# Layer 1's experts in two 64-column halves with 68 streamed columns, issued two experts ahead

## The reference, cut to what matters

```python
E = 32; K = 2; CF = 1.2; D = 128; F = 512
C = int(math.ceil(T * K / E * CF))                  # 68 slots for each expert
xe = jnp.zeros((E, C, D), x.dtype).at[flat_e, pos_d].add(x_rep, mode='drop')
he = jax.nn.gelu(jnp.einsum('ecd,edf->ecf', xe, w1) + b1[:, None, :], approximate=False)
ye = jnp.einsum('ecf,efd->ecd', he, w2) + b2[:, None, :]
y_flat = ye[flat_e, jnp.minimum(pos, C - 1)] * valid[:, None].astype(x.dtype)
y = (y_flat.reshape(T, K, D) * w[..., None]).sum(axis=1)
```

## Time and profile before

| | us |
|---|---|
| median of 3 runs | 669.22 |
| lowest, highest | 668.12, 670.95 |
| span of the profiled execution, first to last instruction | 666.6 |
| median less that span | 2.6 |
| PE busy | 527.9 (79%) |
| DVE busy | 386.9 (58%) |
| ACT busy | 328.5 (49%) |
| POOL busy | 219.3 (33%) |
| first L1667 matmul starts | 571.98 |
| last L1677 matmul ends | 639.36 |

### The profile page before, as it was taken

The page is one execution under the profiler, slowest core; times in us unless marked ns, Lnnn a source line. Parts: engine busy times, 40 slices in busy tenths (PEclk is TensorE's granted clock), DMA queues, the critical chain, the costliest instruction groups (busy, mean ns, idle before and its releaser), DMA issues.

```text
span 666.6 us, 15622 instructions
## 1 busy us (share of the span) xinstructions
PE 527.9 (79%) x5272; PEld 403.1 (60%) x5272; DVE 386.9 (58%) x1148; ACT 328.5 (49%) x953; POOL 219.3 (33%) x409
## 2 busy tenths in 40 slices
PE   2968878876879996999999998999997720799930
PEld 1623245544744535788888887888886420799930
DVE  1699845557365543777877877787786350122212
ACT  2646734344121223887787877778785210222210
POOL 8384722124100000534344443444433016000025
PEclk9798977899868997999999999999999575699985
DMA  9985543333199925000004999000001971200012
GB/s 275 232 236 144 156 155 110 98 113 92 33 233 225 207 72 224 2 2 3 1 0 107 228 230 179 2 2 1 0 0 32 425 304 51 68 17 17 17 36 67
DMA packets 46839, 73.32 MB, mean 110 GB/s; under 512 B 4613, under 2 KB 40374, under 8 KB 45638
## 3 DMA queue, kind: packets, MB, share of 16 engines
q1 hardware_dynamic: 42588, 59.93, 35.9%
q0 software_dynamic: 1472, 8.72, 3.6%
q10 hardware_dynamic: 2730, 4.03, 2.0%
HBM read 69.06 MB, written 3.60 MB: 109 GB/s over the span
## 4 chain that ended last, share of the span: by engine, by line
PE 49%; DVE 20%; ACT 11%; DMA 6%; issue 6%; POOL 6%; POOLq 1%; ACTq 0%; SPq 0%; DVEq 0%
PE ps L1541 9%; ACT work L833 6%; PE ps L1555 5%; PE ps L1677 4%; PE ps L1478 4%; PE ps L1667 4%; DMA work<-in_kv_blk 3%; PE ps L1512 2%; PE ps L1586 2%; POOL xe_scratch L720 2%; DVE ps L1164 2%; DVE sumsq L958 2%; POOL early_w L725 2%; PE ps L1415 2%; PE ps L1358 2%
## 5 line engine op out<-in xcount | busy, mean ns | idle before, releaser
L833 ACT ACTIVATE work<-ps,nb,rkey 125x56 f32<-125x56 f32 x576 | 176.3, 403 | 52.1 <-DVE nb L1167 44.9
L1541 PE MATMUL ps<-work,region 128*64 128x96 f32 (+1 forms) x2304 | 116.7, 252 | 7.0 <-DVE work L1227 4.8
L1541 PEld LDWEIGHTS ps<-work,region 128*64 128x64 f32 (+1 forms) x2304 | 99.5, 137 | 18.7 <-issue 5.2
L1555 PE MATMUL ps<-region,work 125*64 125x129 f32 x1152 | 72.5, 273 | 4.6 <-POOL work L686 3.1
L686 POOL TENSOR_TENSOR work<-work,rs 125x336 f32<-125x336 f32 x96 | 71.9, 749 | 7.5
L1555 PEld LDWEIGHTS ps<-region,work 125*64 125x64 f32 x1152 | 64.1, 136 | 5.4 <-POOL work L686 3.6
L684 POOL TENSOR_TENSOR rs<-rs,rkey 125x6 f32<-125x6 f32 x96 | 19.2, 201 | 123.8 <-DVE rs L1179 123.8
L1164 DVE TENSOR_REDUCE ps<-ps 125x6 f32<-125x336 f32 x96 | 48.9, 510 | 17.9 <-PE ps L1541 17.4
L1175 DVE TENSOR_REDUCE sm<-work 125x6 f32<-125x336 f32 x96 | 47.4, 494 | 1.2 <-ACT work L833 0.6
L725 POOL DMA_INDIRECT early_w<-ys_scratch,gidx x14 | 13.4, 958 | 83.3 <-DMA ys_scratch<-folded 79.4
L1386 PE MATMUL ps<-xln,folded 128*128 128x448 f32 x64 | 29.9, 592 | 9.5 <-ACT region L760 9.5
(11 more groups left out here) (296 smaller groups left out, 1037.9 us busy)
## 6 DMA issues: line engine op xcount, KB each, us to landing
region<-in_w SPq DMA_DIRECT2D x6, 2048.0 KB, 19.5
region<-in_ctxT SPq DMA_DIRECT2D x16, 750.0 KB
early_w<-in_ctx SPq DMA_DIRECT2D x16, 672.0 KB
region<-in_ctx SPq DMA_DIRECT2D x16, 672.0 KB
work<-in_ctxT_blk SPq DMA_DIRECT2D x22, 187.5 KB
early_w<-in_w POOLq DMA_DIRECT2D x1, 4096.0 KB, 12.4
region<-in_ctx_blk ACTq DMA_DIRECT2D x11, 187.5 KB
early_w<-in_ctx_blk ACTq DMA_DIRECT2D x10, 187.5 KB
```

The lines of the kernel that those rows point to most:

```text
L833: i = act.activation(shares_of(a, h)[:, c, :], ps[:CP, 2 + 2 * a + h, c * S:(c + 1) * S], ACT.Exp, bias=nb[:, a, q:q + 1], scale=rkey[:, b ...
L1541: mm = pe.matmul(ps[r0:r1, 2 + 2 * a + h, c * S:c * S + WIDE], keysT[:, s, c0 + r0:c0 + r1], qT[:, p, a * S:a * S + WIDE], start=True, sto ...
L1555: mm = pe.matmul(ps[i * COL:(i + 1) * COL, bank, 0:KW], A[:CP, i, h, c * S:c * S + COL], keys[:, 2 * p + i, h * CH + c, :], start=(h == 0 ...
```

## The change

The weights of both products are split in two column halves: each matmul becomes two of 64 weight columns, the first writing PSUM partitions 0 to 63 and the second 64 to 127. Each streams the expert's own 68 columns, so the zeroed pads and POOL's three memsets and the wait for them (`wide_ok`) go. `hidden` runs two experts ahead in three banks (0, 1, 4), and the order is the same for all experts. The transposed token chunks use banks 5 and 7. DVE's sum of a group is taken out two experts later, and `slot_rows` and its copy stand two experts later as well. DVE's and ACT's instructions keep their shapes.

```diff
+HBANK = (0, 1, 4)
+XBANK = (5, 7, 5, 5, 5)
@@ POOL
-            gp.wait_ge(ln_out, 8)
-            gp.memset(xeT[:, SLOTS:], 0.0).then_inc(wide_ok, 1)
-            for k in range(2):
-                gp.memset(hT[k][:, FC * CAP:], 0.0).then_inc(wide_ok, 1)
@@ ACT
-                    if slot_rows_after(c) + 2 == e:
+                    if slot_rows_after(c) + 4 == e:
                         slot_rows(c)
@@ DVE
-                v.tensor_tensor(hx[e % 2][:, :, :], ps[:, e % 2, 0:FC * CAP]...
+                v.tensor_tensor(hx[e % 2][:, :, :], ps[:, HBANK[e % 3], 0:FC * CAP]...
-                if e % 4 == 3:
-                    g = e // 4
-                    v.wait_ge(ye_mm, e + 1)
+                if e % 4 == 1 and e > 4 or e == E1 - 1:
+                    g = e // 4 - (e % 4 == 1)
+                    v.wait_ge(ye_mm, 4 * g + 4)
@@ PE expert_rows
-                    pe.wait_ge(xe_ev, c - 1)
+                    pe.wait_ge(xe_ev, c)
@@ PE hidden
-                    pe.wait_ge(wide_ok, 3)
-                pe.wait_ge(xe_ev, min(YC, (e * CAP + WIDE - 1) // 512 + 1))
-                if e >= 2:
-                    pe.wait_ge(h_b, e - 1)
+                pe.wait_ge(xe_ev, ((e + 1) * CAP - 1) // 512 + 1)
+                if e >= 3:
+                    pe.wait_ge(h_b, e - 2)
                 for c in range(FC):
-                    mm = pe.matmul(ps[:, e % 2, c * CAP:c * CAP + WIDE], weights(e)[:, c * 128:(c + 1) * 128],
-                                   xeT[:, e * CAP:e * CAP + WIDE], start=True, stop=True)
+                    for r0 in (0, COL):
+                        mm = pe.matmul(ps[r0:r0 + COL, HBANK[e % 3], c * CAP:(c + 1) * CAP],
+                                       weights(e)[:, c * 128 + r0:c * 128 + r0 + COL],
+                                       xeT[:, e * CAP:(e + 1) * CAP], start=True, stop=True, skip_group_check=True)
@@ PE result
-                    mm = pe.matmul(ps[:, 2 + g % 2, e % 4 * CAP:e % 4 * CAP + WIDE], weights(e)[:, F1 + c * 128:F1 + (c + 1) * 128],
-                                   hT[e % 2][:, c * CAP:c * CAP + WIDE], start=(c == 0), stop=(c == FC - 1))
+                    for r0 in (0, COL):
+                        mm = pe.matmul(ps[r0:r0 + COL, 2 + g % 2, e % 4 * CAP:(e % 4 + 1) * CAP],
+                                       weights(e)[:, F1 + c * 128 + r0:F1 + c * 128 + r0 + COL],
+                                       hT[e % 2][:, c * CAP:(c + 1) * CAP], start=(c == 0), stop=(c == FC - 1), skip_group_check=True)
@@ PE order
             hidden(0)
+            hidden(1)
             for e in range(E1):
-                if e + 1 < E1 and e % 4 != 3:
-                    hidden(e + 1)
+                if e + 2 < E1:
+                    hidden(e + 2)
                 result(e)
-                if e + 1 < E1 and e % 4 == 3:
-                    hidden(e + 1)
...
-                    if slot_rows_after(c) + 1 == e:
+                    if slot_rows_after(c) + 3 == e:
                         slot_rows(c)
```

More of the change, by code:

```diff
@@ L173, in build_program @@
         trash = sb("trash", [128, TOP1, NT])
-        hT = [sb(f"hT{k}", [128, FC * CAP + WIDE - CAP]) for k in range(2)]
+        hT = [sb(f"hT{k}", [128, FC * CAP]) for k in range(2)]
         hx1 = sb("hx1", [128, FC, CAP])
@@ L258, in build_program @@
         ysr = folded[:, 2 * T:2 * T + SLOTS].rearrange("p (n d) -> p n d", n=ST)
-        xeT = ln_tiles[:, 0:SLOTS + WIDE - CAP]
-        hx = [ln_tiles[:, SLOTS + WIDE - CAP:SLOTS + WIDE - CAP + FC * CAP].rearrange("p (c n) -> p c n", c=FC), hx1]
+        xeT = ln_tiles[:, 0:SLOTS]
+        hx = [ln_tiles[:, SLOTS:SLOTS + FC * CAP].rearrange("p (c n) -> p c n", c=FC), hx1]
         used["work"] = 0
@@ L402, in build_program @@
         tok_ev = sem("tok_ev")
-        wide_ok = sem("wide_ok")
         xe_mm = sem("xe_mm")
@@ L885, in expert_rows @@
                 act.wait_ge(xe_mm, c + 1)
-                act.copy(xeT[:, 512 * c:512 * c + w], ps[:, 4 + c % 2, 0:w]).then_inc(xe_ev, 1)
+                act.copy(xeT[:, 512 * c:512 * c + w], ps[:, XBANK[c], 0:w]).then_inc(xe_ev, 1)
             expert_rows(0)
@@ L905, in _ @@
                 for c in range(YC):
-                    if slot_rows_after(c) + 2 == e:
+                    if slot_rows_after(c) + 4 == e:
                         slot_rows(c)
             for c in range(YC):
-                if slot_rows_after(c) + 2 >= E1:
+                if slot_rows_after(c) + 4 >= E1:
                     slot_rows(c)
@@ L1322, in _ @@
                     v.wait_ge(h_ok, e - 1)
-                v.tensor_tensor(hx[e % 2][:, :, :], ps[:, e % 2, 0:FC * CAP].rearrange("p (c n) -> p c n", c=FC),
+                v.tensor_tensor(hx[e % 2][:, :, :], ps[:, HBANK[e % 3], 0:FC * CAP].rearrange("p (c n) -> p c n", c=FC),
                                 bcast(b1T[:, e, :], CAP), ALU.add).then_inc(h_b, 1)
-                if e % 4 == 3:
-                    g = e // 4
-                    v.wait_ge(ye_mm, e + 1)
+                if e % 4 == 1 and e > 4 or e == E1 - 1:
+                    g = e // 4 - (e % 4 == 1)
+                    v.wait_ge(ye_mm, 4 * g + 4)
                     v.tensor_tensor(ysT[:, 4 * g * CAP:4 * (g + 1) * CAP].rearrange("p (c n) -> p c n", c=4),
@@ L1644, in expert_rows @@
                 if c >= 2:
-                    pe.wait_ge(xe_ev, c - 1)
+                    pe.wait_ge(xe_ev, c)
                 for j in range(4 * c, min(4 * c + 4, ST)):
-                    mm = pe.transpose(ps[:, 4 + c % 2, j % 4 * 128:(j % 4 + 1) * 128], xe[:, j, :], ident[:, :])
+                    mm = pe.transpose(ps[:, XBANK[c], j % 4 * 128:(j % 4 + 1) * 128], xe[:, j, :], ident[:, :])
                 mm.then_inc(xe_mm, 1)
@@ L1700, in _ @@
                 for c in range(YC):
-                    if slot_rows_after(c) + 1 == e:
+                    if slot_rows_after(c) + 3 == e:
                         slot_rows(c)
             for c in range(YC):
-                if slot_rows_after(c) + 1 >= E1:
+                if slot_rows_after(c) + 3 >= E1:
                     slot_rows(c)
```

## The result

| | before | changed |
|---|---|---|
| median | 670.09 us (4 runs) | 634.74 us (4 runs) |
| lowest, highest | 668.12, 674.0 | 633.56, 638.57 |
| span of the profiled execution | 666.6 | 633.3 |
| first hidden product starts | 571.98 | 570.04 |
| last result product ends, by the timeline | 639.34 | 606.12 |

The ratio is 0.9495, with a 95% interval of 0.9453 to 0.9536. The forecast was 640.3 us with a range of 637.0 to 652.5: right in direction and in mechanism, but the time lies 2.3 us under the range.

What follows compares the result with a forecast made beforehand. PE's expert-stage matmuls bound the kernel: slow start 6.6, pairs 26.9, transposes 2.3, switches 1.65, stall 0.35, copies 0.4, drain 0.25 make 38.5 us against 67.38, so the median falls from 669.22 to 640.3 us; range 637 to 652.5.

Steps and rivals of the forecast that it cites:

- PE bounds the stage: Expert stage: PE stays the bound, needing 0.95 us per expert against 0.6 for DVE and 0.6 for ACT.
- The price of a pair: Expert products: two 64-column matmuls with 68 streamed columns start every 0.059 us at full clock; 456 pairs take 26.9 us.
- The lower bound: Expert products: a pair can't go below 0.056 us, half of a 128-column load, if the halves load beside each other.
- The rule on loads: Expert products, rival: halves sharing all rows load and stream in series, 0.115 us a pair, 669 us; chance 0.07 with another.
- Switches: Expert stage: going between 128-column transposes and 64-column products costs 0.33 us a round trip, five trips 1.65 us.
- Stalls: Expert stage: PE's waits for gelu go with hidden two experts ahead; 0.35 us remains at the last expert.
- The 0.4 us on ACT's copies: Expert stage: allowance for six chunk copies on ACT standing ahead of a gelu, 0.4 us in all.
- The slow start: Start of the expert stage: clock stays at 1.2 GHz for 6.6 us, as before, and 56 of 512 pairs pass.
- the attention's 3.7 us: Attention: clock rose about 3.7 us behind the first pair; if so in the expert stage, 1.4 us less.
- The part ahead of the stage: Everything before the expert stage: taken as unmoved, so the stage's 28.9 us come straight off the span.
- The 2.6 us between span and median: Whole kernel: the median's 2.6 us above the profiled span stay, so span 637.7 us gives median 640.3 us.
- The rival on the clock: Expert stage: shorter streams keep the clock at 1.2 GHz, stage 66.9 us, median 669 us; chance 0.07 shared with another way.

Runs made afterwards that it cites:

- e5: Changed kernel with 48 instead of 68 streamed columns, the last 20 slots of each expert not computed; stage 35.4 us, ratio to the kernel before 0.9558.
- e8: Changed kernel with unread filler matmuls ahead of the stage, gelu table loaded early and two transpose visits fewer; stage 35.4 us, ratio to the kernel before 0.9468.
- r_before: The kernel before, unedited, run again for a second profile; stage 65.5 us, clock rise after 2.3 us, ratio 0.9953.
- e1: Changed kernel with whole 128-column weights instead of halves, still 68 streamed columns; 715.65 us, stage 113.5 us, ratio to the kernel before 1.0734.
- e4: Changed kernel with whole 128-column weights and 96 streamed columns, pads back, so only the new order remains; stage 60.7 us, ratio to the kernel before 0.9918.
- e7: e1 with unread filler matmuls ahead of the stage and the gelu table loaded early; 659.04 us, stage 59.4 us, ratio to the kernel before 0.9860.
- e9: e8 with four filler matmuls instead of two after the last scatter; stage 34.4 us, ratio to the kernel before 0.9485.
- e6: Changed kernel with eight unread 128x448 filler matmuls ahead of the stage and the gelu table loaded early; 634.59 us, stage 35.0 us, ratio to the kernel before 0.9482.

## Why the prediction came out as it did

**PE bounds the stage.** Right: no gap in 20 us, DVE and ACT at half.

**The price of a pair, 0.059 us.** Right: 0.0592. Three rows at 96, 128 and 129 columns, continued to 68, were exact. The lower bound, half of a 128-column load, was off: 0.0583 measured (e5), not 0.056, which would have mattered with fewer columns.

**The rule on loads.** The Trainium skill (page "TensorE: Matmul & The Clock Gate", section "The mechanism") says in its list of what overlaps that a load overlaps matmuls in flight only between different row groups. By it the stage would have stayed near 67 us. The halves share all rows, and 0.0592 us a pair holds two loads and two streams, which in series would take 0.115 by the prediction's prices; the measurement decides against the rule in that form. The same section also names a background weight buffer as a case in which a load is pulled ahead, and with that the measured pair agrees.

**Switches, 0.33 us a round trip.** Right: 0.3 by e8.

**Stalls.** Right: they went, but for 0.35 us at the last expert. The 0.4 us on ACT's copies was not there: the products run on without a gap.

**The slow start.** This is the step of the sum that failed: "I leave that moment where it is: 6.6 us". The clock rose after 3.0 us, and 3.6 x (1 - 0.059/0.114) = 1.7 us of the 2.4 by which the stage beat my 38.5 us are that. The 6.6 us were no property of the kernel before (2.3 in r_before), and all eight other profiles with a rise inside the stage and no fillers ahead have 2.3 to 3.3. I had the attention's 3.7 us as a second reading and used it only as an end of the range. The rest of the 2.4 is the 0.4 us for copies and 0.3 of rounding and small terms.

**The part ahead of the stage.** I took the stage's gain off the median as if nothing else moved. The profiled stage began 1.9 us earlier than before. No edit reaches what lies ahead of the attention, and the start of the stage wanders: over 14 profiles the first hidden product starts between 564.5 and 575.3 us, and the attention's first matmul between 253.0 and 261.3 us. So single medians differ by some us for that alone. The kernel before's two profiles are late in that spread (572.0, 575.3) and the changed kernel's three earlier (570.0, 567.6, 572.8). Most of that spread is there before the attention begins: from its first matmul to the stage it is 311.2 and 314.0 us in the kernel before and 311.4, 312.8 and 312.5 in the changed one. The kernel before's two profiles are the latest of the 14 at the attention as well. Five profiles don't tell whether that is chance, and I leave it open.

**The 2.6 us between span and median.** I kept them as if they were fixed. An execution's time was 1.7 to 1.9 us above its span in the profiles where both are on record; the rest of the 2.6 was that the profiled execution of the kernel before was faster than the median. In the changed kernel the median is 1.4 us above the profiled span. The 5.6 us by which the median came in under the forecast are 2.4 in the stage, 1.9 ahead of it, 1.2 in this difference and 0.1 behind the stage. So the slow start is the largest single term of the stage's sum that was wrong, but with it put right the forecast would still have been some 4 us too high.

Together: stage 31.3 us less by the first pair of profiles, 29.4 with early rises in both (65.5 and 36.1), and the sum said 28.9. The three ratios of the changed kernel, 0.9495, 0.9520 and 0.9529, are 33.8, 32.1 and 31.5 us of 669 to 670; their intervals reach down to 28. The forecast was 3 to 5 us short of these, and they lie 2 to 4 us above the 29.4 that the stages give; how much of that is a later rise in executions of the kernel before, and how much the part ahead, stays open. The range was cut at 637, 3.3 us below the forecast, of which the 1.4 us of an early rise were the only part with a reason. Nothing stood for the spread of the part ahead, which alone is wider.

**The rival on the clock.** I gave it one sentence ("the clock stays at 1.2 GHz, as the streams are shorter") and dismissed it for this form. That was right for the halves, in part by luck: the row that it rested on streams 96 columns, and no row had 68. It is exactly what happens with the whole weights (e1). It was the largest effect near this change: 68 columns with 128-column loads cost 48 us, with 64-column halves the change gave 29 to 31 in the stage.

## What to carry to other kernels

Where float32 matmuls stand further apart than their streamed columns need, the weight load bounds them: write them as two 64-column halves to different PSUM partitions, which load and stream side by side, and only then narrow the stream. Don't narrow the stream behind a 128-column load first, and look at the granted clock, not at PE's busy share, after any such edit. When products get faster, count how many of them now cover the path over the other engines, since the order was worth twice as much here after the halves as before them. A time of a clock change that comes from one profile is a draw, not a constant.

## What the runs showed of the hardware that I had not expected

- PE busy for all of 80 us at a granted 0.50: loads of 128 float32 columns with 68 streamed ones didn't raise the clock in 113 us; with 96 streamed ones it rose after 2.3 us; with 68 it stayed at 1.00 for 59.4 us once it had risen during fillers (e1, e4, e7; one profile each).
- Two 64-column halves side by side, with 48 streamed columns, start a pair every 0.0583 us (e5), where one load of 128 columns keeps records 0.112 apart.
- A visit of 128-column transposes amid 64-column pairs costs 0.3 us beside its own matmuls (e8 against the changed kernel, e9 against e6).
- With PE idle for 2.3 us ahead of the stage the clock fell at its start, with 0.8 us it did not (e8, e9); one profile each.
